# Eigenvector solve of a four-layer graph network on one Trainium2 core: its own stage taken apart and spread over three later stages

## What is computed

```python
deg = A.sum(0) + A.sum(1) - diag(A)
s = where(deg > 0, rsqrt(deg), 0)
L_norm = s[:, None] * (diag(deg) - A) * s[None, :]
_, U = eigh(L_norm)                     # 64 x 64
agg = einsum('mn,bnd->bmd', U.T, x)
out = relu(agg @ W1 + b1) @ W2 + b2
return einsum('nm,bmd->bnd', U, out)
```

## Time and profile before

| | us |
|---|---|
| median of 3 runs | 2178.49 (2175.26 to 2181.86) |
| the profiled execution | 2178.28 |
| its span, first to last instruction | 2176.5 |
| mean granted TensorE clock | 0.948 of full |
| busy: TensorE / VectorE / ScalarE / GpSimd | 1945.8 / 1499.8 / 1142.6 / 737.4 |

### The profile page before, as it was taken

The page is one execution under the profiler, slowest core; times in us unless marked ns, Lnnn a source line. Parts: engine busy times, 40 slices in busy tenths (PEclk is TensorE's granted clock), DMA queues, the critical chain, the costliest instruction groups (busy, mean ns, idle before and its releaser), DMA issues. The chain is left out here.

```text
span 2176.5 us, 32907 instructions
## 1 busy us (share of the span) xinstructions
PE 1945.8 (89%) x11835; PEld 1652.8 (76%) x11835; DVE 1499.8 (69%) x3937; ACT 1142.6 (52%) x1800; POOL 737.4 (34%) x1921
## 2 busy tenths in 40 slices
PE   4999777999999999999999707998969899699996
PEld 4999665788889999988888606886769844388996
DVE  5766455666656676888888785656856568698675
ACT  2444445554445454544444305765757488566675
POOL 3333224343544554000000007646644200006775
PEclk9999789999999999999999957999979999899998
DMA  3110101000100000000000005311222100003122
GB/s 99 49 40 1 39 0 39 1 0 1 39 1 1 1 1 1 1 1 1 1 0 1 1 1 159 117 59 49 87 68 69 49 1 1 10 1 119 40 68 87
DMA packets 65632, 71.16 MB, mean 33 GB/s; under 512 B 3767, under 2 KB 63294, under 8 KB 65470
## 3 DMA queue, kind: packets, MB, share of 16 engines
q1 hardware_dynamic: 65470, 69.07, 9.9%
HBM read 43.90 MB, written 25.17 MB: 32 GB/s over the span
## 5 line engine op out<-in xcount | busy, mean ns | idle before, releaser
L916 ACT ACTIVATE l_gates<-l_acc,l_b 128x512 f32<-128x512 f32 (+1 forms) x504 | 300.2, 633 | 98.1 <-PE l_acc L507 95.8
L505 PE MATMUL l_acc<-l_x_hi,l_w1x_hi 128*128 128x336 f32 (+1 forms) x544 | 192.7, 354 | 41.6 <-ACT l_gates L916 29.8
L923 ACT ACTIVATE l_gates<-l_cell 128x512 f32<-128x512 f32 (+1 forms) x144 | 83.9, 582 | 258.4 <-DVE l_cell L989 145.3
L897 ACT ACTIVATE l_x_hi<-hT 128x512 fp32r<-128x512 f32 (+1 forms) x144 | 100.9, 753 | 175.5 <-PE l_acc L507 167.4
L506 PE MATMUL l_acc<-l_x_hi,l_w1x_lo 128*128 128x336 f32 (+1 forms) x544 | 192.1, 353 | 0.0
L507 PE MATMUL l_acc<-l_x_lo,l_w1x_hi 128*128 128x336 f32 (+1 forms) x544 | 192.1, 353 | 0.0
L505 PE MATMUL l_acc<-l_x_hi,l_w0x_hi 128*128 128x512 f32 x464 | 181.0, 390 | 0.6 <-ACT l_gates L916 0.4
L506 PE MATMUL l_acc<-l_x_hi,l_w0x_lo 128*128 128x512 f32 x464 | 180.6, 389 | 0.0
L507 PE MATMUL l_acc<-l_x_lo,l_w0x_hi 128*128 128x512 f32 x464 | 180.6, 389 | 0.0
L209 POOL TENSOR_SCALAR bi_shifted<-bi_shifted 32x1 f32<-32x1 f32 x62 | 28.7, 463 | 442.0 <-DVE bi_shifted L199 441.9
L1244 POOL MEMSET n_power<- 128x4 f32 x1 | 0.1, 106 | 441.5 <-POOLq L2179 441.5
(11 more groups left out here) (504 smaller groups left out, 6264.9 us busy)
## 6 DMA issues: line engine op xcount, KB each, us to landing
xin<-in_x SPq DMA_DIRECT2D x16, 512.0 KB, 3.8
hidB<-in_x SPq DMA_DIRECT2D x16, 512.0 KB, 4.8
x<-hT SPq DMA_DIRECT2D x16, 512.0 KB, 3.1
hidB<-x SPq DMA_DIRECT2D x16, 512.0 KB, 3.8
x<-hidB SPq DMA_DIRECT2D x16, 512.0 KB, 2.9
attention_residual<-x SPq DMA_DIRECT2D x16, 512.0 KB, 3.9
out_x<-hT SPq DMA_DIRECT2D x16, 512.0 KB, 3.0
l_rawx<-in_wih SPq DMA_DIRECT2D x4, 1024.0 KB, 4.8
```

Of the source, the lines that this page charges most:

```text
L505: t.matmul(out, left[0], right[0], start=start, stop=False)
L897: i = a.activation(as_windows(xs[s % 2][0][:, ch, 0:bg * nw], nw), cols(p, bg, nw, group, k, ch), ACT.Copy)
L916: i = a.activation(gates[:, j, q, 0:n], acc[:, j, q, 0:n], FUNC[q], bias=b[:, o:o + 1])
L923: a.activation(tcell[:, j, 0:n], cell[:, j, 0:n], TANH).then_inc(tc, 1)
```

## The change

The stage `eigenvectors` is gone. A class `Eigenvectors` holds what is left of it:

- The pivots of both ends run as one chain, the second end in partitions 64 to 127 with its order reversed, two instructions a step. `begin` and the first five steps stand in group 3 of the convolution, five more in each group up to 14, and three in group 15, behind `rows_in` and ahead of the hidden statistics.
- The rest is cut into eight pieces, which VectorE does behind the stacks of batches 8, 11, 15, 16, 19, 23, 24 and 27 of the edge attention. The norm's inverse root is a power and one Newton step on GpSimd. The largest eigenvalue comes by a 32x32 transpose on VectorE in place of the matmul.
- The products with Q, the copies and the high and low parts of U and UT stand in the loop of the attention matrices: transpose and copies ahead of product 0, two matmuls ahead of product 3, ScalarE's high parts behind product 4, VectorE's low parts ahead of product 6. ScalarE fills the four tiles with zeros at the stage's start.
- `basis2` and `basis_t2` are gone from the constants, with their two fills.

```diff
-            for name in ("adj_t2", "adj2", "basis2", "basis_t2"):
+            for name in ("adj_t2", "adj2"):
                 pool.memset(c[name][:, :], 0.0).then_inc(filled, 1)
-            pool.wait_ge(filled, 6)
+            pool.wait_ge(filled, 4)
...
-def eigenvectors(nc, sem, c, bi):
...
+class Eigenvectors:
...
+    def begin(self, v, s):
+        lam, rows, lo, up = self.bi.lam, self.bi.rows, slice(0, N), slice(N, P)
+        s.add(v.tensor_copy(self.coupling[lo, 1:], rows[lo, 2, 1:]))
+        s.add(v.tensor_copy(self.coupling[up, 1:], rows[up, 2, N - 1:0:-1]))
+        s.after(v.tensor_scalar(lam[:, 7:8], lam[:, 4:5], 0.5 * F, lam[:, 3:4], ALU.mult, ALU.add))
+        s.add(v.tensor_scalar(self.shifted[lo, :], rows[lo, 0, :], lam[lo, 7:8], None, ALU.subtract))
+        s.after(v.tensor_scalar(self.shifted[up, :], rows[up, 0, ::-1], lam[up, 7:8], None, ALU.subtract))
+        s.after(v.tensor_copy(self.pivot[:, 0:1], self.shifted[:, 0:1]))
+
+    def step(self, v, s, j):
+        n = slice(j + 1, j + 2)
+        s.after(v.reciprocal(self.inverse[:, j:j + 1], self.pivot[:, j:j + 1]))
+        s.after(v.tensor_scalar(self.pivot[:, n], self.inverse[:, j:j + 1], self.coupling[:, n], self.shifted[:, n],
+                                ALU.mult, ALU.add))
...
+        elif n == 2:
+            s.add(v.tensor_scalar(top_inv[:, 0:N - 1], self.inverse[lo, 0:N - 1], 1e18, -1e18, ALU.min, ALU.max))
+            s.after(v.tensor_scalar(bottom_inv[:, 1:], bottom_inv[:, 1:], 1e18, -1e18, ALU.min, ALU.max))
+            s.add(v.scalar_tensor_tensor(over[:, 0:N - 1], top_inv[:, 0:N - 1], -1.0, e[:, 1:N], ALU.mult, ALU.mult))
+            s.after(v.scalar_tensor_tensor(under[:, 1:N], bottom_inv[:, 1:], -1.0, e[:, 1:N], ALU.mult, ALU.mult))
+            s.add(v.tensor_tensor_scan(above[:, ::-1], over[:, ::-1], hit[:, ::-1], 0.0, ALU.mult, ALU.add))
+            s.after(v.tensor_tensor_scan(below, under, hit, 0.0, ALU.mult, ALU.add))
+        elif n == 3:
+            s.after(v.tensor_tensor(zt, above, below, ALU.add))
+            s.after(v.tensor_tensor(zt, zt, hit, ALU.subtract))
+            s.after(v.tensor_tensor(g, zt, zt, ALU.mult))
+            v.tensor_reduce(self.scalars[:, 0:1], g, AX.X, ALU.add).then_inc(squares, 1)
+            s.add(v.tensor_copy(col[:, 0:1], lam[0:32, 7:8]))
+            s.after(v.tensor_copy(col[:, 1:2], lam[32:N, 7:8]))
+            s.after(v.transpose(row, col.unsqueeze(2).to_broadcast([32, 2, 32])))
+            s.after(v.tensor_reduce(sg[0:32, 5:6], row, AX.X, ALU.max, apply_absolute_value=True))
+            s.after(v.tensor_copy(sg[32:N, 5:6], sg[0:32, 5:6]))
...
                     if g + 3 < GROUPS:
                         rows_in(g + 3)
+                    if g == 3:
+                        pivots = Seq(dve, ev_chain)
+                        ev.begin(v, pivots)
+                    if g >= 3:
+                        for j in range(5 * (g - 3), min(5 * (g - 2), N - 1)):
+                            ev.step(v, pivots, j)
...
+        EV_AT = {8: 0, 11: 1, 15: 2, 16: 3, 19: 4, 23: 5, 24: 6, 27: 7}
...
                 pool.memset(apad[:, :, :], 0.0).then_inc(zero, 1)
+                ev.inverse_norm(nc.gpsimd, Seq(pool, ev_pool), squares).then_inc(norms, 1)
...
+                    if j in EV_AT:
+                        ev.part(v, dve, vectors, EV_AT[j], c["ones"][0:N, 0:N], squares, norms)
...
+                    if i == 4:
+                        act.wait_ge(bases, 1)
+                        act.wait_ge(zeroed, 4)
+                        for basis, ps in ((U, ps_u), (UT, ps_ut)):
+                            for h in (slice(0, N), slice(N, P)):
+                                a.activation(basis[0][h, h], ps[h, :], ACT.Copy).then_inc(u_hi, 1)
...
+                for n in range(2):
+                    v.tensor_copy(Q2[:, n * N:(n + 1) * N], ev.bi.QT[:, :]).then_inc(z_copied, 1)
+                dve.wait_ge(z_done, 1)
+                for n in range(2):
+                    v.tensor_copy(Z2[:, n * N:(n + 1) * N], ps_z).then_inc(z_copied, 1)
                 for i in range(PRODUCTS):
+                    if i == 6:
+                        dve.wait_ge(u_hi, 4)
+                        for basis, ps in ((U, ps_u), (UT, ps_ut)):
+                            for h in (slice(0, N), slice(N, P)):
+                                v.tensor_tensor(basis[1][h, h], ps[h, :], basis[0][h, h].bitcast(F32), ALU.subtract).then_inc(u_lo, 1)
...
+                t.transpose(ps_z, ev.signed[:, :], c["ident"][0:N, 0:N]).then_inc(z_done, 1)
                 for i in range(PRODUCTS):
                     u = i % DEPTH
+                    if i == 3:
+                        pe.wait_ge(z_copied, 4)
+                        t.matmul(ps_u, Q2[:, :], Z2[:, 0:N], start=True, stop=True)
+                        t.matmul(ps_ut, Z2[:, :], Q2[:, 0:N], start=True, stop=True).then_inc(bases, 1)
...
-        stage(eigenvectors, c, bi)
+        ev = Eigenvectors(ctx, nc, bi)
```

More of the change, by code:

```diff
@@ new lines, in __init__ @@
+        self.bi = bi
+        self.shifted, self.coupling, self.pivot, self.inverse = (sb("ev_" + n, [P, N]) for n in (
+            "shifted", "coupling", "pivot", "inverse"))
+        self.signed, self.scalars = sb("ev_signed", [N, N]), sb("ev_scalars", [N, 8])
+    def begin(self, v, s):
[6 more added lines that the diff above has]
+        s.after(v.tensor_copy(self.pivot[:, 0:1], self.shifted[:, 0:1]))
@@ new lines, in step, with place, inverse_norm @@
+    def step(self, v, s, j):
[3 more added lines that the diff above has]
+                                ALU.mult, ALU.add))
+    def place(self, w):
+        self.w = [w[:, n * N:(n + 1) * N] for n in range(12)]
+        self.g = w[:, 12 * N:12 * N + 32]
+        self.few = w[0:32, 13 * N:14 * N]
+    def inverse_norm(self, p, s, squares):
+        x, y, t = self.scalars[:, 0:1], self.scalars[:, 1:2], self.scalars[:, 2:3]
+        s.eng.wait_ge(squares, 1)
+        s.after(p.memset(self.scalars[:, 4:5], -0.5))
+        s.after(p.tensor_tensor(y, x, self.scalars[:, 4:5], ALU.pow))
+        s.after(p.tensor_scalar(t, y, y, x, ALU.mult, ALU.mult))
+        s.after(p.tensor_scalar(t, t, -0.5, 1.5, ALU.mult, ALU.add))
+        return p.tensor_scalar(self.scalars[:, 3:4], y, t, None, ALU.mult)
@@ L1696, in edge_attention @@
         ps_s = [ctx.enter_context(nc.psum_tensor(f"sc_s{i}", [P, E], F32)) for i in range(2)]
+        ev.place(xq[0:N, 6 * E:8 * E])
+        ev_chain, ev_pool, squares, norms = (sem("ev_" + n) for n in ("chain", "pool_chain", "squares", "norms"))
+        EV_AT = {8: 0, 11: 1, 15: 2, 16: 3, 19: 4, 23: 5, 24: 6, 27: 7}
         score, top, tops, ex, run, tot = (xq[:, n * E:(n + 1) * E] for n in range(6))
@@ L1784, in _ @@
                 PER = PER_Q // BATCH
+                vectors = Seq(dve, ev_chain)
                 for j in range(1, B // BATCH):
@@ L1846, in _, with attention_and_spectral @@
                 turn(QUARTS - 1)
-def attention_and_spectral(nc, sem, c, m, attn, res, place, hT, hid, x2, wo_t, w1, b1, w2, b2, out):
+def attention_and_spectral(nc, sem, c, m, ev, attn, res, place, hT, hid, x2, wo_t, w1, b1, w2, b2, out):
     DEPTH, RES, BIAS = 4, 2, BIAS_ROWS
@@ L1895, in attention_and_spectral @@
         cleared, w_in, w_hi, w_lo = (sem("as_" + n) for n in ("cleared", "w_in", "w_hi", "w_lo"))
+        ps_z, ps_u, ps_ut = ps_o[0][0:N, 0, 0:N], ps_o[1][:, 0, 0:N], ps_o[1][:, 2, 0:N]
+        z_done, z_copied, bases, zeroed, u_hi, u_lo = (sem("ev_" + n) for n in ("z", "z_copied", "bases", "zeroed", "u_hi", "u_lo"))
         built, summed, by_act, by_dve = (sem("nw_" + n) for n in ("pair", "summed", "act_copied", "dve_copied"))
@@ L1981, in high @@
                     a.activation(part_of, source, ACT.Copy).then_inc(w_hi, 1)
-                high(U[0][:, :], c["basis2"][:, :])
-                high(UT[0][:, :], c["basis_t2"][:, :])
-                act.wait_ge(cleared, 3)
+                act.wait_ge(cleared, 4)
+                for basis in U + UT:
+                    a.activation(basis[:, :], zero[:, :], ACT.Copy).then_inc(zeroed, 1)
                 high(ones[:, :], ones_raw[:, :])
@@ L2206, in network @@
                   nc.sbuf_tensor("attn_lo", [P, EC, QUARTS * P], F32R) as attn_lo):
-                stage(edge_attention, c, m, xq, a["acol"], (attn_hi, attn_lo))
-                stage(attention_and_spectral, c, m, (attn_hi, attn_lo), res, place, hT, xq, x2, a["wo_t"], a["sw1"], a["sb1"],
+                stage(edge_attention, c, m, ev, xq, a["acol"], (attn_hi, attn_lo))
+                stage(attention_and_spectral, c, m, ev, (attn_hi, attn_lo), res, place, hT, xq, x2, a["wo_t"], a["sw1"], a["sb1"],
                       a["sw2"], a["sb2"], out)
```

174 lines of the change are left out of this document (62 added, 112 removed).

## The result

The changed kernel takes 2128.94 us (median of four runs, 2124.19 to 2129.46), the kernel before 2179.03: a ratio of 0.9766, 95% interval 0.9746 to 0.9787. Five more runs of it beside nine of the kernel before gave 2129.10 and 0.9768 (0.9754 to 0.9781). The forecast was 2123.8 with a range of 2120 to 2131; the median lies in the range, but outside the 2121 to 2126.5 to which the forecast itself gave 0.68. The stage is gone and most of its time stayed gone; 5 us that the sum did not have came in. The profiled execution took 2129.12 us (span 2127.3), where the sum gave 2123.6.

The account below looks back on a forecast made before the run. The prediction took the serial VectorE stage `eigenvectors`, overlapped by nothing, as the stretch to remove. Terms -55.43 - 0.28 (two memsets) + 0.3 + 0 + 0.7 = -54.7 from 2178.49 gave 2123.8 us, range 2120 to 2131.

Parts of the forecast that it names:

- The stage that goes: Serial VectorE stage `eigenvectors` between LSTM and convolution: its whole interval, barrier included, leaves the path, -55.43 us.
- The pivots: Convolution: steps of 0.42 us fit VectorE's waits except in group 3, where `begin` adds; +0.3 us, between 0 and 1.3.
- each of the two instructions has a row of its own size: Convolution pivots: reason for 0.42 us a step, from old-chain times of 0.17 (reciprocal) and 0.24 (multiply-add).
- The room: Convolution, steady group: VectorE's idle time that pivot steps can fill, 2.83 us against a need of 2.1.
- Pivots slowed by GpSimd: Rival, convolution: sharing SBUF with GpSimd stretches a step to 0.67 us, giving 2130 us; chance 0.13.
- The pieces: Edge attention: VectorE's added pieces delay no stack that TensorE needs; 0, from above +2 us if one is late.
- The tightest place is between batches 15 and 17: Edge attention: pieces 2 and 3 go there, with 4.1 us of room before TensorE starts batch 17's stack.
- The bases: Attention-matrix loop: only VectorE's four subtractions before product 6 are paid, 0.17 us each; +0.7 us, between 0.4 and 1.0.
- The two matmuls behind sum 2 cost TensorE at most: Attention-matrix loop: at most 1.1 us at half clock, half that at full clock, with VectorE the later engine there.
- The clock: Convolution's start: half clock as before; full clock may return up to 4 us sooner or later, 0 +-2 us.

Follow-up runs that it names:

- p_stt: Changed kernel plus 32 unawaited TensorE semaphore increments, with the pivot's multiply-add as one scalar_tensor_tensor with one pointer scalar: a step 0.46 us in place of 0.51.
- pad32: Changed kernel plus 32 TensorE semaphore increments nobody waits for, ahead of the edge attention's last turn: 2122.45 us, ratio 0.9752.
- p_edge: Changed kernel plus 32 unawaited TensorE semaphore increments, with pieces 0, 1 and 2 together at batch 15 of the edge attention: 2128.34 us.

## Where the prediction was right and where it failed

**The stage that goes** (-55.43): right, and nothing of it came back as a wait of the same kind. The table load, the row and the copies were inside it.

**The pivots** (0.42 us a step, +0.3): the mechanism was right, the size was off. A step is 0.51, `begin` 1.46 and not 1.0, over my upper bound of 1.35. The 0.42 took the old row of 0.24 us, a `scalar_tensor_tensor` over 64 partitions, for a `tensor_scalar` with two pointer scalars over 128. The step that failed was "each of the two instructions has a row of its own size": the new form had none. The second pointer scalar is 0.05 of the missing 0.09. The rest is that both old rows (0.17 and 0.24) are the second of a pair, while a lone reciprocal and a lone multiply-add take 0.20 and 0.26 to the next start (`p_stt`, 1308.21 to 1308.67). The room was a little larger than counted (3.05 for 2.83), 2.53 us fitted into groups 4 to 12 by either, and group 3 paid: +1.2 in this loop, near its upper bound, of which +0.4 is left at the first gather.

**Pivots slowed by GpSimd**, the likeliest rival: did not happen. The instruction, with one tensor input, is equally long beside an idle and a busy GpSimd; only the two-tensor form of `p_stt` stretched. Its time, 2128 to 2130, is close to what was measured, and that is chance.

**The pieces** (0): right for the time, 3.11 us against 3.3 and TensorE started on the stack 1.0 us behind its end. "The tightest place is between batches 15 and 17" was loose: batch 16 has 2.4 us.

**The bases** (+0.7): mis-sized, +1.9. "The two matmuls behind sum 2 cost TensorE at most" half of 1.1 us, "and VectorE is the later one there", put them at 0; TensorE's products are 0.77 us longer just there, in each profile with the change. That is read from the places of the matmuls; no run leaves them out. A subtraction takes 0.25 us of VectorE's time and not 0.17: 1.01, my upper bound. Moving the subtractions gave 1.3 us back, part of it in the twenty products behind them, which the prediction had left as they were; how four subtractions slow those is open.

**The clock** (0 +-2): the range was right and both signs occurred: -1.6 in the last LSTM steps, +1.3 in the last stretch. That last stretch took 148.2 to 153.7 us in all profiles. In the changed kernel the clock is at 0.50 from 1984 to 1994, in `pad32` it is back at 1.00 within 5 us of the same place. This explains a spread of 4 us between executions; what decides it is open.

**What was missing** was a term for TensorE's own instruction stream. The prediction counted instructions by their durations, never by their position, and "0" stood for the whole stretch behind the matrix loop. It held +4.5 of the +5.5 us between 2123.6 and 2129.12; the rest is the matrix loop (+1.2 over its term), the convolution (+0.1) and the clock (-1.6 and +1.3). The change moved the border of a block by only four matmuls in this stream (110th to 114th); what hurt is that the refill came 8 us late, 1.9 of them because of two 512 KB loads and the rest for a reason that stays open. None of my rivals had it; the range held the time by luck, because of rivals that did not happen.

**Still open**: the increments made the hole rare, one profile in seven, but did not exclude it, and the two slow times of `pad32` may be it. In the profile of `p_edge` a q8 packet lies at 1845.5, just behind the stage's start (as in the changed kernel, at 1843.4), and the next two at 1879.7 and 1912.0; in `pad32` it lies at 1840.8, ahead of the start, and the next at 1870.3, 1900.6 and 1912.0. So an execution can be in either of two sequences of refills, and the increments shift the odds. Why was not found.

## What to carry to other kernels

A wait that the profile puts down to "issue" inside a dense stream of small matmuls was here the instruction stream running dry: look at the instruction packets by DMA queue and at the bulk loads issued just ahead of it. A change that adds or removes instructions on an engine can make or heal such a hole, so compare stretches between the same instructions before a difference of a few microseconds is put down to the edit. For a latency chain, take a price only from a row with the same form and the same number of pointer operands, and put work that nobody needs soon behind a busy loop, not into it.

## What the runs showed that was not expected

- 128 matmuls of 64x64 pass in 2.10 us; a refill packet that came ahead of the loads was followed by work 2.9 us later (1908.4 to 1911.26), so a late refill leaves a hole even with no traffic ahead of it.
- An idle stretch of 3.3 us on TensorE in mid-stream went with a granted clock of 0.50, the lower of its two levels, for 6.8 us, and the one of 1.97 us with 0.50 for 3.4.
- A semaphore increment on TensorE costs some 0.15 us, nine times the spacing of these small matmuls (2.10 us for 128).
- A second pointer scalar costs 0.05 to 0.06 us on a 128x1 VectorE instruction (273 ns against 220, and against 212 for L383).
- A 128x1 instruction with two tensor inputs stretched now and then beside a busy GpSimd, from 220 to 285 and once 678 ns; the one with one tensor input never did.
- Copies out of PSUM on VectorE grew from 1.25 to 1.5 us in single rounds, some of them while ScalarE copied without a pause. The kernel before has such a round too (1.44); no run takes the cause apart.
